# All probability-value products of a windowed attention added by VectorE, attention output turned and projected in pairs of chunks, two result banks for the experts all along

## The chip, the cores and the metric

One NeuronCore of one Trainium2 chip. The metric is the device time of one execution in microseconds (us); lower is better. The kernel before has a median of 1211.37 us over three runs (1206.40 to 1219.11).

## The reference

`x` is 8192 tokens (32 sequences of 256) of 128 float32 channels. Three sublayers follow one another:

```python
x = x + 0.5 * moe(layernorm(x))       # 8 experts 128 -> 512 -> 128, exact gelu, top 2 by softmax
x = x + attention(layernorm(x))       # 16 heads of 8 channels
x = x + 0.5 * moe(layernorm(x))       # the same weights again
```

The attention is windowed: a token looks at itself and the 8 tokens before it in its sequence. For each of the 9 window places `w` and each head, a score is the sum of 8 products `q * k`, the softmax runs over the 9 places, and the output is the sum over the 9 places of probability times value; the result is multiplied by `Wo` (128x128) and added to `x`.

## The kernel before

**Layout.** The tokens lie in four groups `g` of 2048 = 128 partitions x `J` = 16. Each partition holds 16 neighbouring tokens, so that the window of a token is found at shifted places of the same partition (and 8 rows carried over), in `qkv`.

**Experts.** A pass of the mixture routes a group (`route`), writes each normalised row to its two experts' regions in HBM (`scatter_rows`, 32 indirect DMAs by POOL for a group, in pass 2 in eight bursts of 4 that each wait until they have landed), makes a plan (`plan`) and then works through tiles of 256 or 128 sorted rows. There are 184 tiles in 7 parts: parts 0 to 3 are the four groups of pass 1 (24 tiles each: 15 of 256 rows, then 9 of 128), part 4 is groups 0 and 1 of pass 2 together (tiles 96 to 135, 31 of them of 256 rows), parts 5 and 6 are groups 2 and 3 of pass 2 (tiles 136 to 159 and 160 to 183). A tile is loaded transposed by SP, multiplied by PE (`up`, L949), passed through gelu by ACT (L756), multiplied again (`down`, L960 and L966) into a result bank, scaled by its gate and taken out by DVE (`take_y`, L1412) and scattered by POOL (L596). `down` of a tile begins with a wait until DVE has taken the earlier result out of that bank. The PSUM banks of the results are given by `Banks((3, 7), (3,), (3, 7))`: banks 3 and 7 in turn in part 0 and in part 6, bank 3 alone in parts 1 to 5. DVE can take tile n out only when tile n - 4 has been scattered, as `y_sb` has four places. A part can begin only when all its rows are scattered and its plan is made, and the rows of a group in pass 2 exist only when its attention has been added.

**Attention of one group** (`attention(g)`), in eight chunks `c` of two rows of tokens per partition, with two product buffers `prod[:, 0:2]` (2304 elements per partition) and two PSUM banks `score_bank` (banks 6 and 7):
- keys: DVE multiplies `q * k` for a chunk (`multiply_keys`, L1151). For chunks 0 to 3 PE adds the 8 channels by eight matmuls with the identity (`add_channels`, L854) and DVE takes the scores (`take_scores`, L1172); for chunks 4 to 7 DVE adds them itself (L1162, L1164).
- softmax: maximum, exponential on ACT, sums and reciprocals, half a group at a time.
- values: DVE multiplies probability and value for a chunk (`prob_value`, L1197). For chunks 0, 2, 4 and 6 PE adds the 9 window places by nine matmuls with the identity (`add_window`, L867); for chunks 1, 3, 5, 7 (`SUMMED_BY_DVE`) DVE does it with four additions (L1206 twice, L1208, L1210).
- output: DVE scales by the reciprocal sums (`take_o`), PE transposes (`turn_o`, L879, 2 transposes), ACT copies (`copy_oT`, L697), PE projects (`project`, L886, 2 matmuls), DVE adds to `x` (`add_attention`, L1243), chunk by chunk. Chunk c uses bank 6 or 7 by its parity.

**What sets the order.** Every engine runs one in-order queue, merged from independent streams by a written-out string each (`PE_ORDER`, `DVE_ORDER`, `ACT_ORDER`, `POOL_ORDER`, `SP_ORDER`). A letter lets one stream take its next step: `r` routing, `e` experts, `a` attention, `p` the preparation of attention (combining a part's results, norm, transposes, q/k/v), `h` the low halves of the rows to scatter; on POOL `s` is a chunk (pass 1) or a burst (pass 2) of row scatters and `y` the scatter of a tile; on SP `t` is a tile's load and `y` the loads of results. If a step has to wait for another engine, everything behind it on its own engine waits too. Below, "y96" means DVE's step for tile 96, and "S5" the row scatters of group 1 in pass 2 (S4 to S7 are groups 0 to 3).

By the strings of before, DVE takes tiles 0 to 43 ahead of the first key multiply; tiles 44 to 62 lie inside attention 0, tiles 63 to 79 inside attention 1, tiles 80 to 95 inside attention 2, tiles 96 to 114 inside attention 3, and tiles 115 to 183 behind it.

Of the kernel before, what the change touches and what calls it, by code (L numbers as in the profile page):

```python
# [24 lines left out]
ALU = mybir.AluOpType  # L25
# [3 lines left out]
P = 128  # L29
# [13 lines left out]
C = 4  # L43
# [16 lines left out]
SUMMED_BY_DVE = (1, 3, 5, 7)  # L60
# [6 lines left out]
    "rrrrrrrrrrrrrrrrrrerrrrrrrrreeeeeeeeeeeeeeeeeeeeeeeeeeeeeeeeeeeeeerreeeeeeeerrrrrrreeeeeeeeeeeeeeeeeeeeeeeeeee"  # L67
    "reeeeeeeeeeeeeeeeeeeeeeeeeeeeeeeeeeeeeeeeeeeeeeeeeeeeeeeepepeeeepepeeeepeeepepeeepeeeepeepeepeepeeepepepaaaaaa"
    "pepepaapepeeeeeeeeeeeeeeeaaaeeeeeeeeeeeeeeeeeeeaeeeeeeeeeeeeeeeeeeeeeeaeaaeepepaapappeepepeaapaaeaaapepaaeaape"
    "aaapepaapaapepaapeaapreaaaaerprpeereeeeeereereereaeereereaeeeeeaeereeaeeeeeeeeeeeeeeeeeaeeeeeaeeeeaappapapepep"  # L70
    "epepaaaapapapappaapaapaaapaapaapppaaaaaaraaeeeereeeeeeeerereeeereeereeeeaaeeaeereeareeeeereeaeeereaaaaaaaaaaaa"
    "aapaappaaapppaappaapppppppppaaaepapraaaeeaeeeeepeeereeeeeeereeeeeeerererererereeeeeeereeaaaeeaeeeeeeeeeeeeeeea"
    "eeeeeeeeaeeeaeaaaeeeeeeaaeaaeaaaeeeaaeaaeaaaeeeeeaaeaaeeeeeeeeerererrerereererereeeeeereeeeeeeeeeeeeeeeeeeeeee"
    "eeeeeeeeeeeeeeeeeeeeeeeeeeeeeeeeeeeeeeeeeeeeeeeeeeeeeeeeeeeeeeeeeeeeeeeeeeeeeeeeeeeeeeeeeeeeeeeeeeeeeeeeeeeeee"
    "eeeeeeeeeeeeeeeeeeeeeeeeeeeeeeeeeeeeeeeeeeeeeeeeeeeeeeeeeeeeeeeeeeeeeeeeeeeee"
)
DVE_ORDER = (
    "rrrrrhrhrrrrrrrrrrrhhrrrrrrrrhhrrrrrhhrhrrrrrrhhhrrrrrererreeeehhhheerrrrherererrrerrereeeeerrrrerererrerhhhee"
    "eeeppehheeppeppepeeeeeehheeeeeeaaaaahaeaaahhheaeaeaaeaaeaaeaeaeppeaaheaeaeppeppeapeaaaahaaeaaaaaeaaaaahaaeaaaa"
    "haaarrareaaaahhaaaeaaeaeaeaeaeaeaearaeraraepperrehhaeaappeppepaahhaaeaaaaaaahhaaaaaaaaaaaaaaarraaraaeahhaaeaea"  # L80
    "aeaaeaeaaeaeaeaaeaeaearererereaaaarahhappaaaaappapphphaaaaaarahaaahraarrraarrrraraaahahaaeaaeaaeaeaaeaaearerre"
    "rrrhhrareraerraeraaeehheaaaaeaaeaaaeaaaaaaaeaaahhaaaeaarrereheererrerrrrerherherrhreeeeeeeeeeeehheeeehheeeeeep"
    "peeppeeeeeeeeeeeeeeepepeepepeepepeepepeeeeeeeeeeepppp"
)
ACT_ORDER = (
    "rrrrrhrrhrrrrrrrrrrrrrrrrrehrrrrhrrrrrrrrhrheeeeeerreeereerreereereeerheeheerreeeeerrrheeeeeereeeeeeeeeeeeheee"
    "eeeeeeeeheeeeeeeeeeeeeppeeeppppeepppeepppeeppheeppepepepeepeppephppephppaeeeeeeeeheeeeeeeeeeeeheeeeeeaeeeeeaap"
    "peeppppppppppeeppaapppeaeappppaappepprrrrehhrrrrrprparpeeereerereerreeeeeereeeeeeeeeeeeaaaeeeehppppppppppppppe"
    "eaappphppppaapppaapppprrrhrrhrrrreeeraeeerereereereeereereeaeeaaraahppaapppppphppppppaapppppppppppeprrrhrrhrrr"
    "eereepaeerpeeeeereeererrrereeeereeeeeeeeeeeaheeaeeeaeeeeaaeeaaeeeheeaaeeerrrhrrrrrreereerrrrerereereheeeeeeeee"  # L90
    "eeeeeeeeeeeeeeeheeeeeeeeeeeheeeeeeeeeeeeeeeeeeeeeeeeeeeeeeeeeeeeeeeeeeeeeeeeeeeeeeeeeeeeeeeeeeeeeeeeeeee"
)
POOL_ORDER = (
    "sssssyysyysyyyyyyyyyyyyyysyyyyyysyyyyyyyyyysyyyyyyyyysysysyyyyysyyyyyyyyyysyyysyyyyyyyyyyyyyssssssssyyyyyyyyyy"
    "yyyyyyyyyyssssssssyyyyyyyysyysyyyysyyyssssyyyyyysyyyyyysyyyyyyyyyyysssyyyyyyyyyyyysyyyyyysssyyyyyyyyyyyyyyyyyy"
    "yyyyyyyyyyyy"
)
SP_ORDER = (
# [61 lines left out]
def macaron(nc, x, Wq, Wk, Wv, Wo, Wg, bg, W1, b1, W2, b2, out):  # L160
# [37 lines left out]
    with ExitStack() as ctx:  # L198
# [412 lines left out]
        def _(act):  # L611
# [89 lines left out]
            def attends():  # L701
                for g in range(G):
                    yield from exponentials(g, 0)
                    yield from exponentials(g, 1)
                    for c in range(CH):
                        yield from copy_oT(g, c)
# [735 lines left out]
```

## Time and profile before

| | us |
|---|---|
| three runs | 1219.11, 1211.37, 1206.40 |
| the profiled execution, its own time | 1195.72 |
| its span (first to last instruction) | 1193.9 |
| its mean granted TensorE clock | 0.898 |
| PE busy / DVE busy / ACT busy / POOL busy | 919.0 / 644.4 / 500.2 / 669.9 |
| first key multiply of attention 0 | starts at 331.37 |
| attention 0, 1, 2, 3 added | at 477.0, 603.6, 731.3, 884.3 |
| last instruction of S5; of S7 | 758; 1092 |

The profiled execution was quicker than each of the three runs. The page gives busy times and a strip of 40 slices; the tables by stretch cut the span at the attentions.

### The profile page before, as it was taken

What the parts mean: (1) busy time and instruction counts of PE and PEld (TensorE: products, weight loads), DVE (VectorE), ACT (ScalarE), POOL (GpSimd) and SP (SyncE); (2) the same over time, 40 slices, a digit from 0 to 9 for tenths busy, and PEclk for the clock granted to TensorE, in tenths of its full rate; (3) what the DMA queues carried; (4) which work ended last, traced back from release to release, by engine and by line L of the source; (5) the groups of instructions that cost most, each with busy time, mean ns of one, the idle gap of its engine ahead of it and who ended that gap; (6) DMA issues with size and microseconds to landing.
All of it is one profiled execution on the core that took longest, in us unless ns stands there. A gap on an engine that the chain in (4) does not pass through costs nothing.

```text
span 1193.9 us, 22506 instructions
## 1 busy us (share of the span) xinstructions
PE 919.0 (77%) x6345; PEld 762.5 (64%) x6345; DVE 644.4 (54%) x1309; ACT 500.2 (42%) x1215; POOL 669.9 (56%) x593
## 2 busy tenths in 40 slices
PE   3446868567897798988898838998988868865984
PEld 3334747456775587777777725677766756754874
DVE  6655133423147587898979998687851511110222
ACT  4433524334534273655644415634434433322432
POOL 2475445446387766455668556356765555555452
PEclk9999769889898799999999978989985988897997
DMA  8813212252113421026112121223222223432683
GB/s 274 235 55 73 55 44 50 65 137 67 42 58 62 134 54 41 19 59 139 33 39 55 23 96 55 45 52 68 50 60 53 51 59 84 116 97 69 154 190 120
DMA packets 170344, 96.44 MB, mean 81 GB/s; under 512 B 137696, under 2 KB 154390, under 8 KB 169332
## 3 DMA queue, kind: packets, MB, share of 16 engines
q1 hardware_dynamic: 152276, 59.29, 21.9%
q0 software_dynamic: 17952, 35.71, 9.5%
q8 instruction: 60, 0.98, 0.4%
q14 instruction: 56, 0.46, 0.1%
HBM read 25.77 MB, written 52.35 MB: 65 GB/s over the span
## 4 chain that ended last, share of the span: by engine, by line
PE 41%; issue 16%; DMA 10%; POOL 9%; another core or an unknown queue 8%; DVE 6%; SPq 6%; ACT 3%; ACTq 0%; POOLq 0%; DVEq 0%
PE bank L966 18%; PE bank L949 12%; POOL x_sorted L579 7%; DMA x_sorted<-hl,slots_all 5%; PE bank L854 3%; DMA x_sb<-in_L_attn_x 2%; PE bank L960 2%; ACT h_f L756 1%; POOL y_pairs L596 1%; SPq L476 1%; PE bank L840 1%; PE bank L867 1%; SPq L466 1%; SPq L452 1%
## 5 line engine op out<-in xcount | busy, mean ns | idle before, releaser
L596 POOL DMA_INDIRECT y_pairs<-y_sb,tile_ids x305 | 359.5, 1179 | 330.0 <-issue 215.9
L756 ACT ACTIVATE h_f<-bank,b_cols 128x256 f32<-128x256 f32 (+1 forms) x736 | 264.1, 439 | 443.3 <-PE bank L949 298.3
L579 POOL DMA_INDIRECT x_sorted<-hl,slots_all x256 | 301.9, 1179 | 179.4 <-issue 86.8
L966 PE MATMUL bank<-w_sb,h_f 128*128 x2440 | 355.2, 299 | 22.6 <-issue 15.3
L966 PEld LDWEIGHTS bank<-w_sb,h_f 128*128 128x128 f32 x2440 | 315.3, 206 | 45.1 <-issue 28.2
L949 PE MATMUL bank<-xsT,w_hl 128*128 128x256 f16 (+1 forms) x2208 | 263.3, 270 | 56.6 <-issue 20.9
L949 PEld LDWEIGHTS bank<-xsT,w_hl 128*128 x2208 | 201.2, 104 | 93.8 <-issue 66.7
L1412 DVE TENSOR_TENSOR y_sb<-bank,tile_ids 128x256 f32<-128x256 f32 (+1 forms) x184 | 68.8, 375 | 342.2 <-PE bank L966 169.0
L960 PE MATMUL bank<-b_hl,ones_b 64*128 x184 | 49.5, 269 | 72.8 <-DVE y_sb L1412 59.8
L960 PEld LDWEIGHTS bank<-b_hl,ones_b 64*128 64x128 f16 x184 | 17.1, 93 | 113.2 <-issue 110.6
L1197 DVE TENSOR_TENSOR prod<-score,qkv 128x2304 f32<-128x2304 f32 x32 | 81.6, 2550 | 0.2
L1151 DVE TENSOR_TENSOR prod<-qkv 128x2304 f32<-128x2304 f32 x32 | 81.4, 2551 | 0.2
L867 PE MATMUL bank<-prod,ident 128*128 128x256 f32 x288 | 67.3, 384 | 2.9 <-DVE prod L1197 2.5
L854 PE MATMUL bank<-prod,ident 128*128 128x288 f32 x256 | 65.4, 413 | 0.4 <-DVE prod L1151 0.4
L685 ACT COPY qkv<-bank 128x384 f32<-128x384 f32 (+1 forms) x96 | 41.3, 450 | 50.1 <-PE bank L840 22.2
L867 PEld LDWEIGHTS bank<-prod,ident 128*128 128x128 f32 x288 | 53.7, 192 | 10.7 <-DVE prod L1197 3.6
L854 PEld LDWEIGHTS bank<-prod,ident 128*128 128x128 f32 x256 | 49.1, 194 | 15.2 <-DVE prod L1151 1.5
L1035 DVE TENSOR_TENSOR hl<-xn_r,hl 128x1024 f16<-128x1024 f32 x24 | 29.3, 1223 | 43.3 <-ACT hl L670 33.9
L840 PE MATMUL bank<-wqkv,xnT_p 128*128 128x384 f32 x128 | 48.8, 509 | 3.5 <-ACT qkv L685 3.5
L670 ACT CAST hl<-xn_r 128x1024 f16<-128x1024 f32 x24 | 24.9, 1044 | 59.4 <-DMA x_sorted<-hl,slots_all 59.4
L614 ACT ACTIVATE xn_r<-x_sb,shift_r,rstd_r 128x128 f32<-128x128 f32 x96 | 39.0, 486 | 10.7 <-DVE shift_r L1022 10.7
L793 PE MATMUL bank<-wg_sb,xnT_p 128*128 128x8 f32 x128 | 27.8, 358 | 8.8 <-issue 5.6
(159 smaller groups left out, 851.3 us busy)
## 6 DMA issues: line engine op xcount, KB each, us to landing
y_in<-y_pairs SPq DMA_DIRECT2D x28, 512.0 KB
x_sorted<-no_rows SPq DMA_DIRECT2D x7, 720.0 KB
y_pairs<-y_sb,tile_ids POOLq DMA_INDIRECT x305
x_sb<-in_L_attn_x SPq DMA_DIRECT2D x4, 1024.0 KB, 5.7
x_sorted<-hl,slots_all POOLq DMA_INDIRECT x256
x_sorted<-no_rows SPq DMA_DIRECT2D x56, 72.0 KB
out<-x_sb SPq DMA_DIRECT2D x3, 1024.0 KB
xsT<-x_sorted SPq DMA_TRANSPOSE x184
```

The lines of the kernel that those rows point to most:

```text
L579: pool.indirect_dma_start(out=x_sorted[p], out_offset=bass.IndirectOffsetOnAxis(ap=slots_all[:, at:at + 1], axis=0), in_=hl[:, c % 2, i // ...
L596: pool.indirect_dma_start(out=y_pairs, out_offset=bass.IndirectOffsetOnAxis(ap=tile_ids[:, t.n % IDS, i, 0:1].bitcast(U32), axis=0), in_=y ...
L756: ins = act.activation(h_part(t, b)[:, k, :], bank[h_banks.uses[u][0]][:, k * t.slots:(k + 1) * t.slots], ACT.Gelu, bias=b1_cols[:, bass.d ...
L840: pe.matmul(prep_bank[k % PREPS][:, 0:3 * D], xnT_p[:, k - RADIUS, 1:1 + P], wqkv[:], start=True, stop=True).then_inc(qkv_done, 1)
L854: ins = pe.matmul(score_bank[c % 2][:, 0:JH * W * HEADS].rearrange("p (n h) -> p n h", h=HEADS), ident[:], products[:, :, d, :], start=(d ...
L867: ins = pe.matmul(score_bank[c % 2][:, 0:JH * D].rearrange("p (j d) -> p j d", d=D), ident[:], prod[:, c % 2, :, w, :], start=(w == 0), st ...
L949: ins = pe.matmul(dst, w1_flat[:, bass.ds((e * HC + c) * (2 * P) + ws * P, P)], slots_of(t)[:, s], start=(n == 0), stop=(n == 2))
L960: pe.matmul(into, ones_b2[:], b2_hl[:, bass.ds(e * D, D)].rearrange("k (o d) -> k o d", o=1) .to_broadcast([2 * B2_LO, t.halves, D]), star ...
L966: ins = pe.matmul(into[:, half, :], h_part(t, c // t.per)[:, c % t.per, half * P:(half + 1) * P], w2_flat[:, bass.ds((e * HC + c) * D, D)] ...
L1151: ins = dve.tensor_tensor(prod[:, prod_of[c]], q_ap.to_broadcast([P, JH, W, D]), windows(lo, D), ALU.mult)
L1197: dve.tensor_tensor(prod[:, c % 2].rearrange("p j w (h d) -> p j w h d", d=DK), score[:, lo:lo + JH].rearrange("p j w (h o) -> p j w h o", ...
L1412: dve.tensor_tensor(y_sb[:, t.ring, 0:t.halves], y_bank(t), tile_ids[:, t.n % IDS, 0:t.halves, 1:2] .to_broadcast([P, t.halves, D]), ALU.m ...
```

## The change

- `SUMMED_BY_DVE` goes: DVE adds the nine window places of all eight chunks, PE's `add_window` is gone (and `pv_summed`). `take_o` always reads `prod`.
- `turn_o`, `copy_oT`, `project` and `add_attention` work on pairs of chunks (`CP` = 4 per group): four transposes, one copy of 512 columns, four matmuls, one addition of 512 columns, all in one bank.
- `score_bank` is bank 6 alone, for the scores of all chunks as well. Bank 7 is thus free, and `y_banks` becomes `Banks((3, 7), (3, 7), (3, 7))`.
- Inside `attention(g)` on DVE the steps stand in another order, and the four strings for PE, DVE, ACT and SP and the one for POOL are written anew.

```diff
-SUMMED_BY_DVE = (1, 3, 5, 7)
+CP = CH // 2
...
-        h_banks, y_banks = Banks((0, 1, 2), (0, 1), (0, 1, 2, 6)), Banks((3, 7), (3,), (3, 7))
+        h_banks, y_banks = Banks((0, 1, 2), (0, 1), (0, 1, 2, 6)), Banks((3, 7), (3, 7), (3, 7))
...
-        score_bank = bank[6:8]
+        score_bank = bank[6]
...
-                act.copy(oT[:, c % 2], score_bank[c % 2][:, JH * D:2 * JH * D].rearrange("p (j n) -> p j n", n=P)
-                         ).then_inc(oT_ready, 1)
+                act.copy(oT[:], score_bank[:].rearrange("p (c j n) -> p c j n", c=2, n=P)).then_inc(oT_ready, 1)
...
                     pe.wait_ge(keys_multiplied, g * C + (c + 1))
-                    if c >= 2:
-                        pe.wait_ge(scores_taken, g * C + (c - 1))
+                    if c >= 1:
+                        pe.wait_ge(scores_taken, g * C + c)
...
-                def add_window(c):
-                    ...
+                def turn_o(i):
+                    pe.wait_ge(o_ready, g * CH + 2 * (i + 1))
+                    if i:
+                        pe.wait_ge(attn_added, g * CP + i)
+                    for j in range(2 * JH):
+                        ins = pe.transpose(score_bank[:, j * P:(j + 1) * P], o_sb[:, j // JH, j % JH, :], ident[:])
...
-                for c in range(0, CH, 2):
-                    for k in (c, c + 1):
-                        if k not in SUMMED_BY_DVE:
-                            yield from add_window(k)
-                    yield from turn_o(c)
-                    yield from turn_o(c + 1)
-                    yield from project(c)
-                    yield from project(c + 1)
+                for i in range(CP):
+                    yield from turn_o(i)
+                    yield from project(i)
...
-                yield from prob_value(1)
                 yield from take_o(0)
                 yield from multiply_keys(7)
                 yield from add_channels(7)
                 yield from subtract_max(1)
+                yield from prob_value(1)
                 yield from take_o(1)
+                yield from prob_value(2)
                 yield from add_attention(0)
-                yield from prob_value(2)
-                yield from add_attention(1)
+                yield from take_o(2)
                 yield from prob_value(3)
+                yield from take_o(3)
                 yield from add_probs(1)
...
+                for i in (1, 2):
+                    yield from prob_value(2 * i + 2)
+                    yield from add_attention(i)
+                    yield from take_o(2 * i + 2)
+                    yield from prob_value(2 * i + 3)
+                    yield from take_o(2 * i + 3)
+                yield from add_attention(3)
```

What the new strings say, counted out step by step: DVE takes tiles 0 to 33 ahead of the first key multiply (before: 0 to 43). Tiles 34 to 62 lie inside attention 0, tiles 63 to 95 inside attention 1, only tiles 96 to 98 inside attention 2 (at its end), tiles 99 to 127 inside attention 3, and tiles 128 to 183 behind it. On POOL, S4.0a now stands behind the scatter of tile 80, and the last four bursts of S4 and all eight of S5 stand in one row behind tile 95 and ahead of tile 96 (before: all of S4 between tiles 75 and 76, all of S5 between 95 and 96). S7 has its first burst behind tile 134, its second behind 135, its third behind 144, and its last five together behind 153 (before: behind 124, then three behind 135, one behind 147, three behind 153). The norm of group 3 for pass 2 and its routing come ahead of tiles 128 to 134.

## Rows read from the trace of the kernel before

**Rows 1.** The page: busy time of PE and DVE, and the granted clock in 40 slices
```profile
PE 919.0 (77%) x6345; PEld 762.5 (64%) x6345; DVE 644.4 (54%) x1309; ACT 500.2 (42%) x1215; POOL 669.9 (56%) x593
...
PEclk9999769889898799999999978989985988897997
```

**Rows 2.** Busy time by stretch, cut at the attentions; stretch, length, engines, clock, DMA share
```profile
331.00:477.00 146.00, 125.07 (x775) 101.11 (x774) 103.11 (x134) 61.59 (x144) 105.59 (x78) 0.91 0.27 69
477.00:604.00 127.00, 117.69 (x790) 95.13 (x788) 112.34 (x176) 73.13 (x176) 70.16 (x48) 0.99 0.26 62
604.00:739.00 135.00, 101.70 (x639) 81.66 (x638) 119.61 (x204) 56.48 (x138) 84.27 (x62) 0.89 0.19 56
739.00:884.00 145.00, 129.21 (x860) 106.72 (x860) 112.07 (x183) 66.08 (x143) 84.88 (x62) 0.95 0.26 53
884.00:1194.00 310.00, 233.44 (x1816) 198.37 (x1814) 70.94 (x191) 109.37 (x299) 158.66 (x159) 0.86 0.39 98
```

**Rows 3.** The same for L1412 alone: tiles taken out by DVE in a stretch
```profile
94.00:331.00 237.00, 16.25 (x43) 0.83 0.28 67
...
739.00:884.00 145.00, 7.92 (x19) 0.95 0.26 53
884.00:961.00 77.00, 5.38 (x13) 0.78 0.21 52
```

**Rows 4.** Groups of instructions by line and shape: busy us, mean ns, idle before
```profile
L1197 DVE TENSOR_TENSOR prod<-score,qkv 128x2304 f32<-128x2304 f32 x32 | 81.6, 2550 | 0.2
L867 PE MATMUL bank<-prod,ident 128*128 128x256 f32 x288 | 67.3, 384 | 2.9 <-DVE prod L1197 2.5 <-DVE x_sb L1243 0.3
L1206 DVE TENSOR_TENSOR prod<-prod 128x1024 f32<-128x1024 f32 x16 | 19.5, 1219 | 0.1
...
L1243 DVE TENSOR_TENSOR x_sb<-bank,x_sb 128x256 f32<-128x256 f32 x32 | 13.5, 420 | 14.7 <-PE bank L886 10.9 <-issue 3.7
...
L1206 DVE TENSOR_TENSOR prod<-prod 128x512 f32<-128x512 f32 x16 | 11.1, 694 | 0.5
L697 ACT COPY oT<-bank 128x256 f32<-128x256 f32 x32 | 11.0, 378 | 22.3 <-PE bank L879 22.2
...
L1208 DVE TENSOR_TENSOR prod<-prod 128x256 f32<-128x256 f32 x16 | 6.8, 425 | 0.5
L654 ACT COPY xnT_p<-bank 128x512 f32<-128x512 f32 x12 | 6.7, 585 | 3.4 <-PE bank L784 1.8 <-remote 0.8 <-issue 0.8
...
L1128 DVE TENSOR_TENSOR x_sb<-qkv,x_sb 128x512 f32<-128x512 f32 x4 | 2.8, 692 | 0.1
```

**Rows 5.** Timeline of PE: `down` of neighbouring tiles, of 256 rows, then of 128
```profile
1113.44 0.28 PE L960 MATMUL bank<-b_hl,ones_b 64*128 x1
...
1116.95 0.28 PE L960 MATMUL bank<-b_hl,ones_b 64*128 x1
...
1171.44 0.23 PE L960 MATMUL bank<-b_hl,ones_b 64*128 x1
...
1173.36 0.23 PE L960 MATMUL bank<-b_hl,ones_b 64*128 x1
```

**Rows 6.** Timeline of POOL: first instructions of neighbouring bursts, in attention 2 and late
```profile
699.07 2.60 POOL L579 DMA_INDIRECT x_sorted<-hl,slots_all  x1 [4.06 <-DMA x_sorted<-hl,slots_all]
...
707.83 0.95 POOL L579 DMA_INDIRECT x_sorted<-hl,slots_all  x1 [2.24 <-DMA x_sorted<-hl,slots_all]
...
1087.12 0.96 POOL L579 DMA_INDIRECT x_sorted<-hl,slots_all  x1 [2.15 <-DMA x_sorted<-hl,slots_all]
...
1094.17 0.99 POOL L596 DMA_INDIRECT y_pairs<-y_sb,tile_ids  x1 [2.31 <-DMA x_sorted<-hl,slots_all]
```

**Rows 7.** Who waited for whom: us in total, times, longest us
```profile
DVE y_sb L1412 <- PE bank L966: 169.0, 71, 10.3
...
PE bank L960 <- DVE y_sb L1412: 59.8, 34, 9.4
...
DVE score L1172 <- PE bank L854: 16.6, 6, 6.2
```

More of the change, by code:

```diff
@@ L72 @@
[L72 to L75, printed above, removed]
+    "rrrrrrrrrrrrrrrrrrerrrrrrrrreeeeeeerrreeeeeeeeeeeeeeeeeeeeeeeeeeeeeeeeeeeeeeeeeeeeeeeeeeeeeeeeeeeeeeeeeeeerrre"
@@ L391, in macaron @@
         SCATTERS = J * DMA
-        def sums_before(g, c):
-            return g * (CH - len(SUMMED_BY_DVE)) + sum(k not in SUMMED_BY_DVE for k in range(c))
         def xt(t, n=1):
@@ L704, in attends @@
                     yield from exponentials(g, 1)
-                    for c in range(CH):
-                        yield from copy_oT(g, c)
+                    for i in range(CP):
+                        yield from copy_oT(g, i)
             def round_weights():
@@ L892, in attention @@
                     yield from add_channels(c)
-                for c in range(0, CH, 2):
-                    for k in (c, c + 1):
-                        if k not in SUMMED_BY_DVE:
-                            yield from add_window(k)
-                    yield from turn_o(c)
-                    yield from turn_o(c + 1)
-                    yield from project(c)
-                    yield from project(c + 1)
+                for i in range(CP):
+                    yield from turn_o(i)
+                    yield from project(i)
             def attends():
@@ L1146, in multiply_keys @@
                         dve.wait_ge(channels_added, g * C + (c - 1))
-                    if c == CH - 1 and 0 not in SUMMED_BY_DVE:
-                        dve.wait_ge(pv_summed, sums_before(g, 1))
+                    if c == CH - 1:
+                        dve.wait_ge(o_ready, g * CH + 1)
                     at.settle()
@@ L1191, in prob_value @@
                     dve.wait_ge(prob_ready, g * 2 + (c // C + 1))
-                    if c >= 3 and c - 2 not in SUMMED_BY_DVE:
-                        dve.wait_ge(pv_summed, sums_before(g, c - 1))
-                    if c - 2 in SUMMED_BY_DVE:
+                    if c >= 2:
                         dve.wait_ge(o_ready, g * CH + (c - 1))
@@ L1201, in prob_value @@
                     yield
-                    if c in SUMMED_BY_DVE:
-                        parts = prod[:, c % 2]
-                        dve.wait_ge(pv_ready, g * CH + (c + 1))
-                        for n in (4, 2):
-                            at.did(dve.tensor_tensor(parts[:, :, 0:n], parts[:, :, 0:n], parts[:, :, n:2 * n], ALU.add))
-                            at.settle()
-                        at.did(dve.tensor_tensor(parts[:, :, 0], parts[:, :, 0], parts[:, :, 1], ALU.add))
+                    parts = prod[:, c % 2]
+                    dve.wait_ge(pv_ready, g * CH + (c + 1))
+                    for n in (4, 2):
+                        at.did(dve.tensor_tensor(parts[:, :, 0:n], parts[:, :, 0:n], parts[:, :, n:2 * n], ALU.add))
                         at.settle()
-                        at.did(dve.tensor_tensor(parts[:, :, 0], parts[:, :, 0], parts[:, :, W - 1], ALU.add))
-                        yield
+                    at.did(dve.tensor_tensor(parts[:, :, 0], parts[:, :, 0], parts[:, :, 1], ALU.add))
+                    at.settle()
+                    at.did(dve.tensor_tensor(parts[:, :, 0], parts[:, :, 0], parts[:, :, W - 1], ALU.add))
+                    yield
                 def add_probs(h):
```

117 lines of the change are left out of this document (41 added, 76 removed).

## The prediction

> **What bounds the kernel now.** I read the page's busy line first: PE 919.0 of 1193.9 us, DVE 644.4 [rows 1]. No engine is full over the whole span, so the averages decide nothing and I went to the table by stretch [rows 2]. It shows two kinds of stretch. In attentions 0, 1 and 3 PE is busy 125 of 146, 118 of 127 and 129 of 145 us with DVE close behind it (103, 112, 112). In attention 2 DVE is the fuller one (119.6 of 135, PE 101.7). Behind attention 3 neither is: PE works 233 of 310 us, DVE 71. There the experts wait for rows: the chain of waits runs over the row scatters S7 and then over PE's tiles. The count of tiles [rows 3] gives the state at each mark: 43 tiles by 331 us, 19 in attention 3, and 13 more until 961. At the end of attention 3 (884) the kernel thus has 69 tiles left. A tile costs PE 3.51 us at 256 rows and 1.92 us at 128 when nothing disturbs it (1116.95 - 1113.44, 1173.36 - 1171.44) [rows 5].
>
> So the end is (time at which attention 3 is added) + (what has to follow it). I work out both.
>
> **What each part removes and adds.**
> - *`add_window` goes.* PE loses 67.3 us of busy time, and since neighbouring groups overlap in that count, 288 passes of 0.216 us = 62 us is what it gives back; a group gets 15.5 us [rows 4].
> - *DVE adds.* Sixteen more chunks, each 1.219 + 0.694 + 0.425 + 0.425 us, with some 0.1 us of settling between them: 2.85 us, 45.6 us in all, 11.4 us a group [rows 4]. The additions wait only for DVE's own multiply. What queues behind them is everything DVE has, `take_y` first.
> - *Pairs.* 32 additions of 0.420 us become 16. One of 512 columns is not in the trace out of PSUM; the nearest row is L1128, 0.692 us out of SBUF, the bounds are 0.42 and 0.84 (one or two of the present ones) and I take 0.69: 13.5 - 11.1 = 2.4 us saved, 0.6 a group [rows 4]. ACT's copies go from 32 x 0.378 to 16 x 0.585 us, 2.7 us saved on an engine at 42%, which is worth nothing. PE's transposes and projections stay in number. DVE in sum: +10.8 us a group.
> - *One bank for scores.* PE may not add chunk c + 1 before DVE has taken chunk c. PE's eight matmuls and DVE's take no longer overlap, some 0.5 us in each of three steps; between 0 and 4 us a group, I take 1.5 (today this wait is 16.6 us in six places [rows 7]).
> - *One bank for a pair.* The last addition of a group now waits for four transposes, a copy and four matmuls with nothing in between (about 6 us; today 10.9 us are waited at L1243 in all [rows 4]). Earlier pairs have a multiply and four additions (5.4 us) as cover; without it, 6 us each. I take +3 us a group, 0 to 12 as bounds.
> - *A second result bank in parts 1 to 5.* PE waits 59.8 us in 34 places for DVE to empty the bank [rows 7]. DVE is in order, so the second bank buys one tile of slack and no DVE time. Bounds 0 and 45 us; I take 22, the middle, as the longer waits (up to 9.4 us) are longer than a tile of slack.
> - *The strings.* They move more than all this. I follow them stage by stage.
>
> **The stages.** *To the first key multiply:* 331.4 us with 44 tiles; now 34 tiles, so 5 x 3.51 + 5 x 1.92 = 27 us less of PE: 304. *Attention 0:* 145.6 us; PE gets those 27 us and loses 15.5, DVE gets 10.8; either way +11.5: 157, ending at 461. *Attention 1:* 126.6 us with 17 tiles; now 33, so PE gets 7 x 3.51 + 9 x 1.92 = 42 and loses 15.5: 117.7 + 26.5 = 144 us of work, DVE 112.3 + 10.8 + 16 x 0.34 = 128.6. PE sets it; with the idle 9 us of today 153, ending at 614. *Attention 2* (to the next key multiply, 135 us): 13 tiles fewer for DVE (-4), +10.8: 126.4 busy, with today's idle 15.4: 142, ending at 756. *Attention 3:* 145.7 us; ten more tiles (+33 us of PE), no `add_window` (-15.5), most of its q/k/v already made in attention 2 (-7): 140 us of PE, 127 of DVE, +13 idle (16 today): 153, ending at 909. With +4.5 us a group for the two single-bank costs, of which I count half since PE-bound stages absorb it (+9), and -22 for the result bank: 896. Before it was 884. The attention part is thus 12 us *later*, but 13 tiles more (12 x 3.51 + 1.92 = 44 us of PE) are done.
>
> *Behind it:* today 69 tiles and 310 us; now 56 tiles. Norm and routing of the last group (PE some 10 us, ACT's 16 activations and 8 copies) and tiles 128 to 135 at 1.92: tile 135 about 33 us after, tile 136 at +48. Tiles 136 to 153 are 15 x 3.51 + 3 x 1.92 = 58 us plus one burst in between, ring waits and the like: +114. Then five bursts of S7 in a row, at 7.05 us each (1094.17 - 1087.12, four issues and the landing) [rows 6]: +149, with a few us more for the data of the last: +151. From the last burst (1092) to the end the kernel takes 102 us, unchanged: +253. The span is 896 + 253 = 1149. The profiled execution's time is 1.8 us over its span, and its 1195.7 lies 15.6 below the median of the runs: 1149 + 1.8 + 15.6 = **1166**, 3.7% under 1211.
>
> **A rule against it.** Row: POOL's scatter instruction that starts beside a VectorE multiply took 2.60 us, one at rest 0.96 [rows 6]. VectorE instructions with two inputs in SBUF thus hold up POOL's indirect DMAs, and the change adds 64 such instructions of 0.43 to 1.22 us. Each can hold at most its own length; most of POOL's have slack.
> The Trainium skill (SBUF — State Buffer, Who interferes with whom) says a two-input `tensor_tensor` contends with GpSimd's reads but infers that descriptor generation is spared; by that the scatters would be unaffected, and the trace disagrees (2.60 against 0.96 us). The price by the row is rival C.
>
> **The rivals.**
> *B, VectorE's work comes fully onto the path.* For it: DVE is within 5 to 22 us of PE in attentions 0, 1 and 3 [rows 2], and an in-order queue rarely overlaps to the last. Then its 10.8 us come on top in those three stages (+32), the single bank's half too (+9): 1207, no change. Against it: PE loses 15.5 us in the same stages.
> *C, slower: the row scatters become the path in attention 2.* Behind tile 95 stand 12 bursts in one row (4 of S4, 8 of S5), and no tile of part 4 can begin before they have landed; ACT's and DVE's rows for S5.2 and S5.3 wait for earlier bursts, and attention 2 waits behind these on DVE. At the pitch of the trace in attention 2, 8.76 us (707.83 - 699.07), they take 105 us, and eight of them behind the gates of group 1 (DVE's 52 us of steps) end at 122 us of a stage of 142: hidden, by some 10 us since tile 96 is needed at about 130. From 9.8 us a burst it decides. If each of the four instructions meets a multiply (2.60 + 0.30, and 2.3 of landing), a burst takes 13.9 us: 52 + 111 = 163, 33 us late, and 12 + 12 more at S4 and S7: +57, 1223. Against it: today one to two in four meet one.
> *D, better overlap.* PE's idle in the four attention stages is 21 + 9 + 33 + 16 = 79 us [rows 2]; if the new order halves it (-39, of which 4 lie in the sum already), 1131.
> *E, the clock.* In attention 2 PE has about 75 us of work in 142. Today's slices go down to 0.6 of full speed, and the stretch 604 to 739 shows 0.89 [rows 1, 2]. If PE ran that stage at 1.2 instead of 2.4 GHz, the 16 us of channel adding and 8 us of turning and projecting, on which DVE waits, would double: +24, 1190.
> The Trainium skill (TensorE: Matmul & The Clock Gate, What's actually happening) says the array's clock is throttled by default and released by activity; it would make this stage the coldest.
> *F, the bank is not what PE waits for* (rings or POOL are): no 22 us, 1188. It lies in the forecast's own range.
>
> **How the numbers follow.** Forecast with F (1140 to 1195): 0.56. D: 0.12. E: 0.06. B: 0.16. C: 0.10. The range reaches from D's 1130, less the noise, to just short of B's far side: 1126 to 1210. Three runs spread by 1%, so 1% is about what can be told. Faster by over 1% (under 1199): forecast, D, E and a few of B: 0.77; within 1% (to 1223): 0.13; slower: 0.10.
>
> **What would show it.** In the profile after: no L867 group; L1206's two shapes x32 each; DVE busy near 688, PE near 857. First key multiply near 304, attention 3 added near 896 with 128 tiles taken, last burst of S7 near 1047. PE's wait for `take_y` at 45 us or less. C is right if POOL's last burst of S5 ends over 130 us after attention 1, with PE idle until then and DVE waiting for `hl`. B is right if DVE is over 95% busy from 304 to the end of attention 3 and that end is past 925. Wrong above all would be the assumption that each stage keeps today's idle time under another order.

## The result: 2 to 3 per cent slower

| | before | after | after / before |
|---|---|---|---|
| first measurement, median us | 1208.88 (1205.74 to 1219.11) | 1245.37 (1232.69 to 1252.18) | 1.024 (1.018 to 1.030) |
| second, a quicker chip | 1079.96 | 1098.91 | 1.019 (1.011 to 1.027) |
| third | 1195.25 | 1230.31 | 1.030 (1.025 to 1.035) |

The ratios compare the quicker group of executions of each kernel, while the medians take in all of them, also 1251.3 and 1252.2 us in the first row and one execution of 1888.5 us in the second.

Forecast were 1166 us, a range of 1126 to 1210, and a chance of 0.10 for slower. The profiled execution of after took 1251.3 us (span 1249.5) against 1195.7 before. Its page begins:

```profile
PE 875.5 (70%) x6057; PEld 713.7 (57%) x6057; DVE 686.6 (55%) x1357; ACT 493.2 (39%) x1195; POOL 650.7 (52%) x593
...
PEclk9998896687997888999978855798988768995997
```

DVE's work changed as counted: +42.2 us (forecast 688, is 686.6). PE has the 288 matmuls less (6345 to 6057), but is busy 875.5 us where 857 were forecast, 43.5 less than in [rows 1] and not 62: its mean granted clock is 0.854, before 0.898. The columns of the next view are those of [rows 2], cut at the first key multiply and where each attention was added (325, 505, 666, 817, 987):

```profile
325.00:505.00 180.00, 136.80 (x941) 111.15 (x939) 117.13 (x155) 72.26 (x177) 111.20 (x88) 0.87 0.25 64
505.00:666.00 161.00, 145.01 (x1057) 116.63 (x1057) 125.69 (x200) 88.97 (x224) 79.05 (x64) 0.96 0.25 58
666.00:817.00 151.00, 77.92 (x354) 54.42 (x353) 130.54 (x210) 46.79 (x104) 67.95 (x55) 0.69 0.18 51
817.00:987.00 170.00, 148.23 (x1068) 123.98 (x1065) 125.04 (x202) 76.00 (x175) 100.58 (x76) 0.92 0.22 51
987.00:1249.00 262.00, 181.52 (x1415) 151.99 (x1415) 65.10 (x178) 87.84 (x239) 133.26 (x133) 0.83 0.41 105
```

The reader is to see that the loss is in no one place. Against the forecast marks (304, 461, 614, 756, 896, end 1149) the first key multiply is 21 us late, and attentions 0 to 3 and the tail take 23, 8, 9, 30 and 9 us longer. 13 of the 30 in attention 3 are bookkeeping: the forecast put its corrections for all four groups (+9 for the single bank, -22 for the result bank) into that last mark. In e13, a quicker execution of the same kernel (1234.5 us), the six differences are 15, 18, 8, 9, 29 and 6 us. In attention 2 PE is busy 78 of 151 us at a granted clock of 0.69. The tiles lie as the strings say, here DVE's y_sb instructions in attentions 1 and 2:

```profile
505.00:666.00 161.00, 11.18 (x33) 0.96 0.25 58
666.00:817.00 151.00, 1.27 (x3) 0.69 0.18 51
```

The groups that answer to [rows 4], and the waits (total us, times, longest) that answer to [rows 7]:

```profile
L1178 DVE TENSOR_TENSOR prod<-prod 128x1024 f32<-128x1024 f32 x32 | 39.1, 1221 | 0.4
...
L1178 DVE TENSOR_TENSOR prod<-prod 128x512 f32<-128x512 f32 x32 | 22.1, 692 | 1.1
...
L1206 DVE TENSOR_TENSOR x_sb<-bank,x_sb 128x512 f32<-128x512 f32 x16 | 10.9, 684 | 8.7 <-PE bank L866 8.7
```

```profile
ACT h_f L749 <- remote: 231.9, 44, 18.5
...
PE bank L830 <- ACT qkv L679: 46.7, 2, 31.5
...
DVE score L1147 <- PE bank L847: 20.1, 9, 3.6
DVE x_sb L1206 <- PE bank L866: 8.7, 5, 4.8
PE bank L935 <- DVE y_sb L1372: 8.3, 5, 4.1
```

The prices of DVE's instructions were right (1221, 692 and 684 ns), and PE's wait for the result bank fell from 59.8 to 8.3 us. What these added up to was not right. The 46.7 us that PE waits for ACT's `qkv` lie in attention 2, where PE idles 73 us in all.

### The profile page after: what moved, and what is told of

The parts are those of the page before. It is cut to its first block and busy times, and to the rows that moved or that the text cites. A ratio compares the mean times of both kernels' runs of the same rounds, so it can differ in the third digit from the quotient of the medians.

```text
span 1249.5 us, 21931 instructions
## 1 busy us (share of the span) xinstructions
PE 875.5 (70%) x6057; PEld 713.7 (57%) x6057; DVE 686.6 (55%) x1357; ACT 493.2 (39%) x1195; POOL 650.7 (52%) x593
## 5 line engine op out<-in xcount | busy, mean ns | idle before, releaser
L590 POOL DMA_INDIRECT y_pairs<-y_sb,tile_ids x305 | 350.5, 1149 | 373.2 <-issue 226.3
L749 ACT ACTIVATE h_f<-bank,b_cols 128x256 f32<-128x256 f32 (+1 forms) x736 | 264.8, 440 | 468.5 <-remote 231.9
L573 POOL DMA_INDIRECT x_sorted<-hl,slots_all x256 | 291.6, 1139 | 211.2 <-issue 126.4
L924 PE MATMUL bank<-xsT,w_hl 128*128 128x256 f16 (+1 forms) x2208 | 267.9, 274 | 105.1 <-ACT h_f L749 54.8
L847 PE MATMUL bank<-prod,ident 128*128 128x288 f32 x256 | 71.8, 434 | 4.0 <-DVE score L1147 3.5
L847 PEld LDWEIGHTS bank<-prod,ident 128*128 128x128 f32 x256 | 51.6, 206 | 20.5 <-issue 3.8
L833 PE MATMUL bank<-wqkv,xnT_p 128*128 128x384 f32 x128 | 52.8, 541 | 13.5 <-ACT qkv L679 13.4
L1178 DVE TENSOR_TENSOR prod<-prod 128x1024 f32<-128x1024 f32 x64 | 61.2, 956 | 1.5
L830 PE MATMUL bank<-wqkv,xnT_p 128*128 128x256 f32 x64 | 21.3, 464 | 48.9 <-ACT qkv L679 46.7
L830 PEld LDWEIGHTS bank<-wqkv,xnT_p 128*128 128x128 f32 x64 | 12.7, 224 | 53.8 <-ACT qkv L679 48.7
```

Of the source, the lines that this page charges most:

```text
L573: pool.indirect_dma_start(out=x_sorted[p], out_offset=bass.IndirectOffsetOnAxis(ap=slots_all[:, at:at + 1], axis=0), in_=hl[:, c % 2, i // ...
L590: pool.indirect_dma_start(out=y_pairs, out_offset=bass.IndirectOffsetOnAxis(ap=tile_ids[:, t.n % IDS, i, 0:1].bitcast(U32), axis=0), in_=y ...
L749: ins = act.activation(h_part(t, b)[:, k, :], bank[h_banks.uses[u][0]][:, k * t.slots:(k + 1) * t.slots], ACT.Gelu, bias=b1_cols[:, bass.d ...
L833: pe.matmul(prep_bank[k % PREPS][:, 0:3 * D], xnT_p[:, k - RADIUS, 1:1 + P], wqkv[:], start=True, stop=True).then_inc(qkv_done, 1)
L847: ins = pe.matmul(score_bank[:, 0:JH * W * HEADS].rearrange("p (n h) -> p n h", h=HEADS), ident[:], products[:, :, d, :], start=(d == 0), ...
L924: ins = pe.matmul(dst, w1_flat[:, bass.ds((e * HC + c) * (2 * P) + ws * P, P)], slots_of(t)[:, s], start=(n == 0), stop=(n == 2))
```

## The experiments

Eighteen kernels ran, on chips of two speeds: on one the kernel before takes 1080 us, on the others 1195 to 1211. Every ratio is to the kernel before on the same chip. e1 to e4 shared a chip, e5 to e8 (the quick one), e9 to e12, e13 to e16, and e17 and e18. The chip of e1 to e4 is that of e13 to e16.

### The four parts of the change, one by one

**e1 and e16: the changed code in the order of before.** DVE's, POOL's and SP's strings of before; PE's and ACT's strings of before without the letters of the steps that are gone, and the first turn of each group some tiles later.

> The changed code (all additions by VectorE, pairs in one bank, two result banks, its own order of attention steps) in the merge strings of the kernel before: its DVE, POOL and SP strings as they stand, PE and ACT without the letters of the steps that no longer exist, and the first transposes of a group (on PE) a few steps later. Theory 'order' (the loss is made by the new strings, above all by an attention 2 that has no tiles beside it): at or under the kernel before, ratio 0.97 to 1.00. Theory 'additions' (VectorE's added 46 us come onto the path whatever the order): 1.02 to 1.04, as the change itself.

> The changed code in the order of before, beside the changed kernel on the same chip. From ratios on different chips (1.039 against 1.019 and 1.024) the new strings are worth 1.5 to 2 per cent: 15 to 25 us above the changed kernel. If it is within 5 us, the ratios of different chips can't be compared that finely, and the strings are worth nothing.

e1: 1242.3 us, 1.039 (1.036 to 1.043). e16: 1237.4, 1.038 (1.033 to 1.042). So the code by itself, with its second result bank, costs nearly 4 per cent in the old order, and the new strings seem to win 0.8 back (1230.3 on the same chip; 15 to 25 us were expected, and the intervals overlap a little).

**e4: only the additions, the rest as before.**

```diff
-SUMMED_BY_DVE = (1, 3, 5, 7)
+SUMMED_BY_DVE = tuple(range(8))
...
+                    if c == CH - 1:
+                        dve.wait_ge(o_ready, g * CH + 1)
```

> The kernel before with one part alone: VectorE adds all eight chunks, each new addition directly behind its multiply, PE's add_window steps gone; banks, pairs and merge strings as before. Theory 'additions': VectorE pays 45 us and PE's 62 us give nothing back: ratio 1.02 to 1.035. Theory 'order': PE's 62 us pay for it where PE is the fuller engine: 0.99 to 1.01.

1225.0 us, 1.025 (1.022 to 1.028): +29 us. PE's 62 us are gone here, and DVE's 42 us added.

**e6: only the relief of PE.** `add_window` does one matmul in place of nine; the other eight places are left out of the sum.

```diff
-                    for w in range(W):
-                        ins = pe.matmul(score_bank[c % 2][:, 0:JH * D]..., prod[:, c % 2, :, w, :], start=(w == 0), stop=(w == W - 1))
+                    pe.matmul(score_bank[c % 2][:, 0:JH * D]..., prod[:, c % 2, :, 0, :], start=True, stop=True).then_inc(pv_summed, 1)
```

> The kernel before with one matmul where add_window has nine (the other eight window places of chunks 0, 2, 4, 6 are left out of the sum); DVE adds what it added. This is the gain of the change, PE relieved of some 55 us, without its price. Theory 1 (PE's time is what the attention stages wait for, as the prediction had it): 30 to 50 us faster, ratio 0.96 to 0.975. Theory 2 (PE's relief comes back as a lower granted clock and idle time, since the stages wait for chains of several engines): within 12 us of before, ratio 0.99 to 1.0, with PE busy down by less than the work taken out and the clock under 0.89.

1077.7 us, 0.999 (0.996 to 1.002). Eight of nine passes are gone, 256 x 0.216 = 55 us of PE by the price of the prediction, and they are worth nothing.

**e7: only the burden of DVE.** As e4, but PE still does its nine matmuls, on other operands:

```diff
-                                        prod[:, c % 2, :, w, :], start=(w == 0), stop=(w == W - 1))
+                                        w2_sb[:, 2 * w:2 * w + 2, :], start=(w == 0), stop=(w == W - 1))
```

> The kernel before with DVE adding the window places of all chunks, and PE still doing nine matmuls of the same shape at the same places (on weights, into the same bank; their result isn't read). So DVE has the price and PE keeps the work. Beside the kernel where DVE adds all and PE's matmuls are gone (1225 us, 29 over before). Theory 1: PE's work costs its length, so this one is 30 to 50 us slower than that, 1255 to 1275. Theory 2: PE's work is nearly free, and this one is within 10 us of it, 1215 to 1235, with a clock of 0.88 or more.

1104.5 us, 1.022 (1.015 to 1.030): +24.6 us, as in e4 within the intervals, with or without PE's work. In columns as above, attentions 0 to 3 of e6 and then of e7. The two differ by DVE's additions and by PE's matmuls; e6 says that the matmuls alone cost nothing there:

```profile
259.00:393.00 134.00, 112.82 (x709) 89.92 (x708) 102.98 (x133) 61.82 (x144) 102.77 (x77) 0.92 0.30 76
393.00:521.00 128.00, 108.98 (x725) 86.95 (x724) 111.63 (x176) 72.51 (x175) 70.72 (x50) 0.93 0.25 62
521.00:647.00 126.00, 81.53 (x556) 65.91 (x554) 113.28 (x188) 52.48 (x127) 77.53 (x57) 0.84 0.20 58
647.00:796.00 149.00, 122.11 (x818) 97.45 (x817) 118.72 (x200) 70.39 (x154) 88.19 (x67) 0.94 0.23 54
```

```profile
261.00:404.00 143.00, 124.15 (x771) 100.78 (x770) 113.42 (x148) 61.57 (x144) 103.25 (x78) 0.93 0.28 72
404.00:541.00 137.00, 121.92 (x790) 98.55 (x789) 123.26 (x193) 73.10 (x175) 70.44 (x51) 0.95 0.25 59
541.00:674.00 133.00, 96.00 (x619) 79.19 (x617) 124.05 (x203) 52.33 (x127) 77.44 (x57) 0.87 0.19 53
674.00:822.00 148.00, 133.30 (x888) 108.57 (x887) 130.25 (x217) 70.11 (x154) 87.48 (x67) 0.98 0.24 55
```

DVE gets 10.4 to 11.6 us more in each, and attentions 0, 1 and 2 grow by 9, 9 and 7. Attention 3 doesn't. Where did PE's relief go? Its waits at `turn_o` within the attentions, in the runs on the quick chip (e7 with PE's work, then e6 without it):

```profile
PE bank L880 <- DVE o_sb L1232: 23.0, 5, 11.2
```

```profile
PE bank L876 <- DVE o_sb L1231: 46.5, 9, 14.1
```

PE reaches `turn_o` earlier and stands there until DVE's `take_o`; in e4, on a slower chip, it stands 64.6 us, in the kernel before on such a chip 23.1. A wait took the place of the work. e7 isn't the clean counterpart, as its matmuls also wait 14.2 us for DVE's `x_sb`, which in before is 0.3 us in one place.

**e8: additions and pairs and one score bank, in the order of before, with one result bank.**

```diff
-y_banks = Banks((0, 1, 2), (0, 1), (0, 1, 2, 6)), Banks((3, 7), (3, 7), (3, 7))
+y_banks = Banks((0, 1, 2), (0, 1), (0, 1, 2, 6)), Banks((3, 7), (3,), (3, 7))
```

> The changed code in the order of before, and with one result bank in parts 1 to 5 as before. Beside the kernel before with all additions on DVE (1225) it differs by pairs of chunks in one score bank and by DVE's order within attention; beside the changed code in the old order (1242) by the second result bank alone. Theory A (the single score bank and the pairs cost, the second bank gains even in the old order): 1260 to 1290. Theory B (the single bank and the pairs cost some 17 us, the second bank is worth nothing in the old order, where it gave 37 in the new): 1237 to 1250.

1131.3 us, 1.049 (1.042 to 1.055): 27 us more than e7 on the same chip, though e7 also has PE's nine matmuls. Neither theory: the second bank is worth about 1 per cent in the old order (e1 and e16 have it, on another chip), and pairs and single bank cost more than thought.

**e10: the same with the scores in two banks. e11: with the pairs in two banks as well.**

```diff
+        score_banks, score_bank = bank[6:8], bank[6]
...
-                    if c >= 1:
-                        pe.wait_ge(scores_taken, g * C + c)
+                    if c >= 2:
+                        pe.wait_ge(scores_taken, g * C + (c - 1))
```

> The changed code in the order of before with one result bank in parts 1 to 5 (1.049 of before), and now the scores of chunks 0 to 3 in two banks in turn, as before the change; the pairs of chunks stay in one bank. If the serial scores (PE adds a chunk's channels only when DVE has taken the chunk before) are what cost the 26 us above the additions, the ratio comes down to 1.025 to 1.03. If it is the output in pairs, it stays at 1.045 or more.

> The same with the pairs in two banks in turn as well, so that the turn of a pair need not wait until the pair before it is added to x. Beside before with all additions on DVE (1.0225 to 1.025) only the pairing and DVE's order within attention are left. If a bank is what is missing, 1.02 to 1.03; if the pairs themselves (the first chunk's output waits for the second's), 1.04 or more.

e10: 1.041 (1.036 to 1.047); e11: 1.044 (1.039 to 1.048). The single bank accounts for 0.5 to 0.7 per cent, across chips and with touching intervals, so no more than likely. Against e4 (1.025), e11 keeps 1.9 per cent with every bank given back.

**e18: e11 with DVE's steps within an attention in the order of before.**

```diff
+                yield from prob_value(1)
                 yield from take_o(0)
...
-                yield from prob_value(1)
                 yield from take_o(1)
...
                 for i in (1, 2):
+                    yield from take_o(2 * i)
+                    yield from take_o(2 * i + 1)
                     yield from prob_value(2 * i + 2)
                     yield from add_attention(i)
-                    yield from take_o(2 * i + 2)
                     yield from prob_value(2 * i + 3)
-                    yield from take_o(2 * i + 3)
```

> The changed code in the order of before with two score banks and one result bank (1.0435 of before), and now DVE's steps within an attention in the order of before as well (prob_value(1) ahead of take_o(0), the take_o of a pair together): what is left against before with all additions on DVE (1.0225 to 1.025) are the pairs alone. If DVE's new order inside attention(g) costs the 19 points, 1.02 to 1.03; if the pairs do (a pair's output, and PE behind it, waits for its second chunk), 1.038 or more.

1.054 (1.046 to 1.061). DVE's new order isn't the cause, if anything it helps. By exclusion the pairs are, together with the places that PE's and ACT's strings give to a pair's steps, which no run separates from them. PE's waits in the attentions of e4 (chunk by chunk) and of e11 (pairs), both in the order of before:

```profile
PE bank L879 <- DVE o_sb L1231: 64.6, 9, 18.0
PE bank L960 <- DVE y_sb L1414: 48.8, 32, 4.6
```

```profile
PE bank L859 <- DVE o_sb L1197: 78.9, 12, 20.8
PE bank L935 <- DVE y_sb L1372: 31.9, 23, 4.5
```

A pair's turn waits for its second chunk, with the tiles queued behind it on PE; DVE then waits for those (`y_sb` <- PE 14.9 us in e4, 23.5 in e11) and for the projection of the pair (`x_sb` <- PE 13.5 and 19.8). This is how the traces read, on two chips and with one execution each; no run shows it by itself.

**e3: the changed kernel with one result bank in parts 1 to 5**, three steps of the strings moved so that nothing deadlocks.

> The changed kernel with one result bank in parts 1 to 5 again (three steps moved by one or two places so that it can run). If the second bank is worth what the fall of PE's wait for it suggests (59.8 to 13.2 us), the time rises by 10 to 25 us, ratio 1.033 to 1.045; if the wait has only moved to ACT's gelu, under 6 us either way.

1286.8 us, 1.076 (1.073 to 1.079), 56 us above the changed kernel on that chip where 10 to 25 were expected; PE's wait for DVE's `y_sb` is 143.1 us. The second bank is the part that the new strings live on.

### What sets the attentions in the new order

**e5 and e13: the changed kernel again**, to stand beside others.

> The changed kernel once more, so that it stands beside the others on one chip. All theories: as measured, 1.01 to 1.03 of before, 1210 to 1235 us where before takes 1196. Its place against the three that follow is what counts, and against the old order: if it is at or under the 1242 us of the changed code in the old order, the new strings cost nothing by themselves and the loss lies in the code; if it is 10 us or more above it, the strings lose.

> The changed kernel beside the three that follow, on one chip: 1.02 to 1.04 of before. Only its place against them counts.

Their times are in the first table.

**e2 and e14: no additions for chunks 0, 2, 4, 6** (left out of the sum; DVE does 42 us less).

```diff
                     dve.wait_ge(pv_ready, g * CH + (c + 1))
+                    if c % 2 == 0:
+                        yield
+                        return
                     for n in (4, 2):
```

> The changed kernel with the four additions of the even chunks left out (the sum of the window is then not made there), 23 us of VectorE work less in all, order and waits kept. Theory 'additions': 20 us or more faster than the change, ratio to the kernel before about 1.00. Theory 'order': VectorE's work is only part of the loss; 10 us or less, ratio 1.015 or more.

> The changed kernel without the additions of chunks 0, 2, 4, 6 (they are left out of the sum): DVE does 42 us less. Theory D (DVE sets the attentions in the new order too, as it does in the old one, where 42 us of additions cost 25 to 29): 17 to 35 us under the changed kernel. Theory P (in the new order 29 to 33 tiles lie in attentions 0, 1 and 3, PE sets those, and attention 2 is set by its own chain): within 8 us of it. The first look, on another chip than the changed kernel, gave 1.038 of before, and DVE's freed time came back as waits.

e2: 1240.7 us, 1.038. e14: 1235.7, 1.033 (1.028 to 1.039), beside 1230.3. Nothing gained.

**e15: four of eight matmuls in each `add_channels`** (half the channels of chunks 0 to 3 are left out). **e17: both cuts.**

```diff
                     for d in range(DK):
+                        if d % 2:
+                            if d % 4 == 3:
+                                yield
+                            continue
                         ins = pe.matmul(score_bank[:, 0:JH * W * HEADS]...
```

> The changed kernel with four of the eight matmuls in each add_channels (half of the channels of chunks 0 to 3 are left out of the scores): PE does some 31 us less in the attentions, and each of the serial steps of the single score bank is shorter by half. Theory P: 15 to 30 us under the changed kernel. Theory D: within 8 us of it.

> The changed kernel with both cuts at once: no additions for chunks 0, 2, 4, 6 (DVE 42 us less) and four of eight matmuls in each add_channels (PE some 31 us less). One cut at a time gave +5 and -5 us, neither told from nothing. If the attentions of the new order are set by two nearly full engines that cover for each other, both cuts give more than their sum: 20 to 40 us under the changed kernel, ratio 0.995 to 1.015 (the changed kernel is at 1.030 on the slower chips, 1.019 on the quicker). If they are set by what these engines wait for (the experts' chain over PE, ACT, the rings and the row scatters), it stays within 10 us: 1.02 to 1.03.

e15: 1225.6 us, 1.025 (1.020 to 1.030). e17: 1229.0, 1.028 (1.021 to 1.035). With 42 us of DVE's and some 31 of PE's work gone (PE is busy 22 us less in the attentions), the four attentions of e17 take 174, 156, 153 and 167 us, against 175, 161, 151 and 169 in e13 on another slower chip: 6 us less in all. So in the new order neither the additions nor the channel matmuls set the end, nor the two in turn. Attentions 0 and 2 of e17 (length, then the engines as in [rows 2]):

```profile
320.00:494.00 174.00, 133.74 (x909) 108.22 (x907) 105.65 (x139) 72.49 (x177) 111.77 (x88) 0.83 0.28 66
...
649.00:802.00 153.00, 73.12 (x320) 50.72 (x319) 119.33 (x194) 46.61 (x104) 70.94 (x55) 0.65 0.17 50
```

In both, PE is idle 40 and 80 us and DVE 68 and 34. What does set them is only read from the traces; no run took it away or moved S5's bursts. In attention 2 it is the chain through the row scatters. Cut at the start of S5's first scatter and at the end of its last, the stage of after is:

```profile
666.00:726.00 60.00, 38.78 (x165) 27.37 (x163) 48.39 (x100) 27.07 (x62) 20.98 (x18) 0.78 0.17 55
726.00:791.00 65.00, 16.94 (x44) 9.90 (x44) 62.81 (x88) 7.87 (x15) 41.74 (x32) 0.55 0.13 44
791.00:817.00 26.00, 22.21 (x145) 17.16 (x146) 19.34 (x24) 11.85 (x27) 5.23 (x6) 0.85 0.30 56
```

In the first 60 us DVE (busy 48) does the norm and routing of group 1, on which S5 waits, among the attention's keys and scores. The additions lie beside the bursts and behind them, so e14 took nothing from the first part, and e17 only some of PE's share. POOL's timeline of after has S5's first scatter, then the first one of the second burst and of the last, and the scatter of tile 96; DVE's has the last addition of attention 1 and tile 96:

```profile
726.58 1.36 POOL L573 DMA_INDIRECT x_sorted<-hl,slots_all  x1 [25.48 <-DVE hl L1021]
...
735.37 1.17 POOL L573 DMA_INDIRECT x_sorted<-hl,slots_all  x1 [2.22 <-DMA x_sorted<-hl,slots_all]
...
784.66 3.13 POOL L573 DMA_INDIRECT x_sorted<-hl,slots_all  x1 [2.15 <-DMA x_sorted<-hl,slots_all]
...
807.77 1.14 POOL L590 DMA_INDIRECT y_pairs<-y_sb,tile_ids  x1 [16.16 <-DVE y_sb L1372]
```

```profile
665.72 0.69 DVE L1206 TENSOR_TENSOR x_sb<-bank,x_sb 128x512 f32<-128x512 f32 x1 [4.83 <-PE bank L866]
...
806.48 0.42 DVE L1372 TENSOR_TENSOR y_sb<-bank,tile_ids 128x256 f32<-128x256 f32 x1 [0.65 <-PE bank L941]
```

A burst takes 8.3 us ((784.66 - 726.58) / 7). DVE took tile 96 out 140 us after attention 1 was added (806.5 - 666.4), and in e5, e13, e14, e15 and e17 139, 140, 146, 139 and 142 us after: a stretch that leaving out work did not shorten. DVE's last steps of attention 2 stand behind tiles 96 to 98 in its queue.

In attention 0 it is likely POOL, on the quick chip at least. POOL's groups in the whole 152 us of attention 0 of e5 (columns: busy us, mean ns, idle before) are:

```profile
L590 POOL DMA_INDIRECT y_pairs<-y_sb,tile_ids x48 | 60.6, 1262 | 14.6 <-issue 14.0 <-DVE y_sb L1372 0.6
L573 POOL DMA_INDIRECT x_sorted<-hl,slots_all x45 | 60.5, 1344 | 18.1 <-issue 18.1
```

That makes 93 scatters at 1.65 us each, busy time and gap. 93 x 0.30 = 28 of the 33 us idle are the plain gap between two scatters, so POOL hardly rests. In e6 it is 77 scatters in 134 us, 23 of 32 us idle. The share of the whole span, 60% in e5, hides it. On the slower chips POOL isn't full there: in after it has 88 scatters in 180 us and is idle 69, of which 26 are the plain gap, beside stalls that the last section tells of. What sets attentions 1 and 3 was not found.

### Two runs beyond the change

**e9: all window places added by PE**, in the code of before.

```diff
-SUMMED_BY_DVE = (1, 3, 5, 7)
+SUMMED_BY_DVE = ()
...
-                        if k not in SUMMED_BY_DVE:
-                            yield from add_window(k)
-                    yield from turn_o(c)
-                    yield from turn_o(c + 1)
+                        yield from add_window(k)
+                        yield from turn_o(k)
```

> The reverse of the change's first part: the kernel before with all eight chunks' window places added by PE (nine matmuls for each of the odd chunks too, placed ahead of the chunk's turn), so that DVE loses its 16 x 2.65 = 42 us of additions and PE gains as much as the change took from it. Theory 2 (DVE's work sets the length of the attentions, PE's work is nearly free): 10 to 30 us faster, ratio 0.97 to 0.99. Theory 1 (PE's work is what they wait for): 30 to 50 us slower, ratio 1.03 or more. A third way: DVE now waits for PE's sum at every odd chunk, and the two cancel, 0.99 to 1.01.

1261.6 us, 1.043 (1.039 to 1.048), though DVE does 42 us less. DVE's waits in the attentions point to why:

```profile
DVE o_sb L1233 <- PE bank L868: 83.5, 18, 7.8
```

`take_o` waits at 18 of 32 chunks for PE's sum, which lies behind tiles in PE's queue. PE is also busy 57 us more (976.4 against 919.0 in before); no run separates the two. "PE's work is nearly free" thus holds for taking it away, not for adding to it: the split of four and four chunks is the best of the three.

**e12: row scatters of pass 1 in fours.**

```diff
-                        if f and (i + 1) % BURST == 0:
+                        if (i + 1) % BURST == 0:
```

> The kernel before with the row scatters of pass 1 held back as those of pass 2 are: after every four indirect DMAs POOL waits until they have landed (no other step moves). In the traces ACT and PE stand idle without a releaser for 7 to 17 us beside eight such DMAs in a row. If these stalls come from the eight in a row and cost the end, 0.97 to 0.99; if they are hidden or the waits of POOL cost as much, 0.995 to 1.01; if POOL is what part 1 waits for, above 1.01.

1208.7 us, 0.997 (0.994 to 1.001). Nothing, and the idle time without a releaser stays (ACT 148.0 us, 131.3 in the trace of before). The eight in a row aren't its cause. No version tried beats the kernel before beyond what a measurement tells.

## Why the prediction was wrong

**The step that failed first** is "DVE gets 10.8; either way +11.5 ... PE sets it": stage by stage, PE's 15.5 us were taken off the stage length and DVE's 10.8 added only where DVE was the fuller. I took the engine with more busy time for the bound. e6 shows the relief at 0 and not some 46 us (three stages of 15.5), e4 and e7 show DVE's 42 to 46 us at 25 to 29, where the sum had them only in attention 2 (+10.8). An in-order queue that others wait on costs whether it is full or not: in e6 and e7 it idles 9 to 31 us in each attention, much of it in waits of a few microseconds for PE and ACT. This is rival B, given 0.16, but only its half on DVE: B put +32 us on attentions 0, 1 and 3, and there e7 over e6 has 9, 9 and -1. B also left PE's 15.5 us a group taken off, and so stopped at 1207; no rival had the relief at nothing. B's own test (over 95% busy) was too hard: in e7 DVE is 79, 90, 93 and 88% busy.

**Pairs and the single bank** stand in the sum with +9 us for the four groups. Measured: 27 us (e8 over e7), some 6 to 9 of them the bank and the rest the pairs. The term priced only DVE's own waits, for scores (16.6 us before, 20.1 after) and at the addition (10.9 before, 8.7 after; in the old order, e8, 18.8). By the traces the larger cost came where the pair's turn stops PE's queue, behind which the tiles stand.

**The second result bank** was taken at 22 us between 0 and 45. It is worth about 1 per cent in the old order (across chips) and 56 us in the new, whose strings were written for it. PE's wait for it, 59.8 us, went to 8.3 as forecast (45 or less). F falls.

**The strings.** Forecast, they carried most of the gain: 27 us before the first key multiply, 57 in the tail. On the quick chip, with e6 for the kernel before (0.999 of it), they gave 259 - 248 = 11 and 276 - 241 = 35 us. By the one comparison that isolates them (e13, e16) they win 7 us. The sum let a stage that is given 12 or 16 tiles more grow by PE's time for them; but these stages wait for POOL or for rows too. This is the assumption that the prediction ended on, that each stage keeps today's idle time, and it failed: attentions 0 and 3 of after idle 43 and 22 us on PE where 21 and 13 were carried over. These parts were measured in different orders and don't simply add up to the miss.

**C, the row scatters as the path in attention 2,** was right in kind and small in size. The burst pitch is 8.3 us (8.76 forecast), S5 ends 125 us after attention 1 (122 forecast, 130 set as the mark). Tile 96 comes at 140 rather than about 130, and the stage takes 151 rather than 142, of which leaving out additions or channel matmuls gives nothing back. Single scatters that ran beside a VectorE multiply took 2.2 to 3.1 us again, one in each of six of S5's eight bursts, against 0.96 at rest. The prediction's rule, "each can hold at most its own length", can be made exact:

```profile
784.39 2.56 DVE L1170 TENSOR_TENSOR prod<-score,qkv 128x2304 f32<-128x2304 f32 x1
784.66 3.13 POOL L573 DMA_INDIRECT x_sorted<-hl,slots_all  x1 [2.15 <-DMA x_sorted<-hl,slots_all]
```

The multiply ends at 786.95, the scatter 0.84 us later. All 88 scatters of after that began inside a VectorE instruction of over 1 us with both inputs in SBUF (at least 0.1 us after its start and 0.2 us before its end) ended 0.83 to 0.88 us after it, while the 14 that began so inside a reduction with one input took 0.95 to 0.99 us, as at rest. A scatter is thus held until the two-input instruction is done. Counted for instructions of 0.4 us and more, this makes a run's scatters longer by 105 us in sum in before, 88 in after and 95 in e13: the change's 64 new additions did not add to it. The Trainium skill (SBUF — State Buffer, Who interferes with whom) infers that descriptor generation is spared by such instructions; this trace disagrees, as [rows 6] did. The row I had already read for attention 2 applied to attention 0 too, where I never asked POOL for its share.

**E, the clock,** came as described, 0.69 in attention 2 and 0.55 beside S5's bursts, and seems not to have mattered: with half the channel matmuls gone (e15, e17) the stage is 150 and 153 us all the same. The turns and projections were not tested. D fell: PE idles 43 + 16 + 73 + 22 = 154 us in the four attentions, not half of 79.

## What to carry to other kernels

Before taking work off the busiest engine, look at who it will wait for next: here 55 to 62 us of matmuls turned into a longer wait at the following step, while the same sums cost 25 to 29 us on the engine that had been idle 46% of the time. Price a moved step by what queues behind its waits on every engine it touches, and for any stage that is given more tiles add up instructions times (busy + issue) for the DMA-issuing engine as well, stage by stage. Merging two small steps into one saves instructions and, as it seems here, costs the earlier step's slack.

## What was not expected of the hardware

The same kernel takes 1080 us on one chip and 1195 to 1211 on the others. The difference is idle time that ends in nothing the profile shows ("remote"): ACT's gelu waits of that kind are 131.3 us in 28 places in the trace of before and 231.9 in 44 in that of after, and none on the quick chip. Their sum varies between executions of one kernel too. In e13, the changed kernel again on a slower chip, they are:

```profile
ACT h_f L749 <- remote: 153.2, 28, 16.9
```

The longest, 16.9 us, ended at 391.7 us in attention 0. 72 of the 122 us between the spans of before and of e6 lie ahead of the first key multiply (331 and 259). On the slower chips the change costs 2.4 to 3.0 per cent, on the quick one 1.9, with intervals that overlap. e12 excludes one cause; what does stall these chips stays open. POOL's scatter costs 0.96 us and 0.30 of issue at rest, and 1.65 us on average in attention 0 of e5. At rest, in after:

```profile
1138.26 0.96 POOL L573 DMA_INDIRECT x_sorted<-hl,slots_all  x1 [0.30 <-issue]
```
